# Attention scores as four products of 32 columns, with 128 columns kept for chunks on the diagonal

## The chip, the cores and the metric

The kernel runs on one core of a Trainium2 chip. The metric is the device time of one execution in microseconds, the median of several runs; less is better. The core has five engines that work at the same time and meet at semaphores: TensorE (PE in the profile; its weight loads are listed apart as PEld), VectorE (DVE), ScalarE (ACT), GpSimd (POOL) and SyncE (SP), whose queue issues most of the DMAs.

## What is computed

The reference is one layer of a decoder on x of 2 x 2048 x 512: attention, cross attention and a feed-forward net. The change lies in the attention. It has 16 heads of 32 in each of two batches, one set of queries, and two sets of keys and values, a short one with a bias and a long one without:

```python
scores = jnp.einsum('bhqd,bhkd->bhqk', q, k) / jnp.sqrt(jnp.float32(hd))
if bias is not None:
    scores = scores + bias[None, None]
attn = jax.nn.softmax(scores, axis=-1)
return jnp.einsum('bhqk,bhkd->bhqd', attn, v)
...
decay_bias = -jnp.abs(pos[None, :] - pos[:, None]) * (1.0 - decay_factor)
out_short = _attention(q, k_s, v_s, decay_bias)
out_long = _attention(q, k_l, v_l, None)
out = alpha * out_short + (1.0 - alpha) * out_long
```

## The kernel before

It runs in four parts, one after the other: `prepare` and `project` (norm, queries, keys and values, and the weights of the feed-forward net), `attend`, and `finish` (output projection, cross attention, feed-forward net). `attend` takes from about 490 us to 3670 us of the span.

`attend` works in **units**. A unit is one head with one set of keys and values: 32 heads in 16 passes of four units, w = 0 to 3. Even units (w = 0, 2) are the short attention with the bias, odd ones the long attention. The 2048 x 2048 scores of a unit are made twice, in f16 with the operands' high and low parts stacked along the contraction (96 rows, with rows for positions and maxima up to 103):

- `scores_for_max` (tile scores_qk, queries on the partitions): 16 tiles of 128 queries, 4 chunks of 512 keys each. VectorE reduces two chunks at a time to row maxima (line 983). Its 64 chunks c are numbered by 4 x tile + key chunk.
- `scores_for_exp` (tile scores_kq, keys on the partitions): 16 blocks of 128 keys, 4 chunks of 512 queries each. The row maximum is subtracted by a further row of the operands; ScalarE takes the exponential of each chunk into probs_T, in f32 (line 961).

`times_v` (line 1143) multiplies a finished block of probs_T by the values, in f32: four products of 32 columns for the four query chunks, each written to its own 32 partitions of outputs_T. The profile shows each f32 product as two records. GpSimd adds up the blocks for the row sums, some by an accumulating DMA; `count` (line 1150) sums them over the partitions by f32 products of 32 columns with ones.

The bias is linear in the positions on each side of the diagonal, with another sign above than below. So an even unit has two query operands, q_operand and q_operand_above (`q_up`), and a piece of a chunk takes the one for its side. `runs` (line 1068) splits a chunk into pieces: a chunk that lies on one side is one product of 512, and a chunk that holds a part of the diagonal has a piece to its left, the 128 x 128 piece on the diagonal, which takes q_operand, and a piece to its right. To the diagonal piece one further product with an identity (scores_qk) or two (scores_kq) add the kink. For tile or block t the diagonal lies in chunk t // 4, so 32 of an even unit's 128 chunks hold a part of it, none of an odd unit's.

The order on TensorE is written out in `one_pass` (line 1189). A unit has 16 **steps**. Step i does the values of block i, in steps 4 and 7 a count for the unit before, and then eight chunks of scores: one of scores_kq, two of scores_qk, two of scores_kq, two of scores_qk, one of scores_kq. The scores_kq chunks of step i are 4i + 7 to 4i + 10, counted on into the next unit from 64 on (`emitted`). The scores_qk chunks are the four of tile (i - 10) mod 16, of the unit after in steps 0 to 9 and of the one after that in steps 10 to 15 (`chunks_of`). scores_kq has three banks in PSUM, scores_qk two pairs of banks; TensorE waits for a bank at lines 1086 and 1089 (VectorE) and 1114 (ScalarE).

The row maxima of the next unit come together in step 10: VectorE reduces and negates them and turns them into rows (line 997), after the first reduction of that step. `place_max` on SP (line 767) then issues the DMAs that write them into the operand rows: eight of 1 KB for an even unit (four for q_operand, four for q_operand_above), four for an odd one. The first scores_kq chunk of the next unit, which is the second scores_kq chunk of step 14, waits for them at line 1120. In an odd unit's steps the next unit is an even one, with eight DMAs.

## Time and profile before

| | us |
|---|---|
| median of 3 runs | 4794.77 |
| lowest and highest | 4790.95 to 4795.98 |
| the profiled execution | 4789.35 |
| its span, first to last instruction | 4787.3 |

The profile is of one execution. Its page lists busy time by engine, the span in 40 equal slices of 120 us (busy tenths, and the granted clock of TensorE in tenths of full speed), the chain that ended last, and the costliest groups of instructions. A timeline gives the start in us, the time to the end of the group, the engine, line, operation and tiles, and how many records are merged; "96*128 96x512" is 96 rows and 128 columns of the stationary operand and 96 x 512 of the moving one, so 128*32 is a product of 32 columns. Records of products are pipelined: they overlap, and the distance between starts is what counts. Starts in a timeline are rounded to 0.01 us.

### The profile page before, as it was taken

To read this page: it belongs to the slowest core of one execution; us is meant where nothing else is said; L and a number is where in the kernel's file an instruction comes from. 1 tells how busy PE (TensorE), PEld (TensorE's weight loads), DVE (VectorE), ACT (ScalarE), POOL (GpSimd) and SP (SyncE) were. 2 spreads that over 40 slices of the span, in tenths; PEclk is the share of its full clock that TensorE was granted. 3 is DMA by queue.
4 is the path that set the end of the run, shared out by engine and by line. 5 is a ranking of instruction groups with operands and counts; after the bars stand their busy time and mean duration, and the time that the engine had idled before them with its cause. 6 is when DMAs were issued, how large, how long until landed. Compare 5 with 4: busy or idle time off the path is not lost. (4 is left out here: it accounts for less than half of the span.)

```text
span 4787.3 us, 95755 instructions
## 1 busy us (share of the span) xinstructions
PE 4623.8 (97%) x30732; PEld 2081.9 (43%) x30732; DVE 3784.0 (79%) x4400; ACT 2984.2 (62%) x5297; POOL 3069.2 (64%) x1236
## 2 busy tenths in 40 slices
PE   8999899999999999999999999999996899999998
PEld 3444233333333333333333333333331677777776
DVE  7657788888888888888888888888881688888887
ACT  3222377777777777777777777777774455555554
POOL 0000388888888888888888888888886233333332
PEclk9999799999999999999999999999998899999999
DMA  5444366766666666767676666666665000000000
GB/s 168 136 126 128 81 147 134 152 137 147 139 147 144 140 144 141 150 137 152 138 150 134 148 143 146 141 143 145 139 131 126 20 21 27 28 25 24 27 23 12
DMA packets 241866, 543.48 MB, mean 114 GB/s; under 512 B 71471, under 2 KB 145327, under 8 KB 200561
## 3 DMA queue, kind: packets, MB, share of 16 engines
q0 software_dynamic: 45792, 333.47, 35.3%
q1 hardware_dynamic: 195563, 203.94, 15.1%
q8 instruction: 258, 4.23, 0.4%
q14 instruction: 215, 1.76, 0.1%
q10 hardware_dynamic: 38, 0.08, 0.0%
HBM read 140.34 MB, written 62.16 MB: 42 GB/s over the span
## 5 line engine op out<-in xcount | busy, mean ns | idle before, releaser
L983 DVE TENSOR_REDUCE rowmax_parts<-scores_qk 128x1 f32<-128x1024 f32 x2048 | 2411.4, 1218 | 549.3 <-PE scores_qk L1066 547.7
L961 ACT ACTIVATE probs_T<-scores_kq 128x512 f32<-128x512 f32 x3840 | 2072.9, 600 | 622.7 <-PE scores_kq L1066 562.1
L868 POOL TENSOR_TENSOR probs_added<-probs_added,probs_T 128x2048 f32<-128x2048 f32 x446 | 2077.1, 4657 | 47.8 <-POOL probs_added L868 44.9
L1066 PE MATMUL scores_kq<-q_operand,k_operand 103*128 103x512 f16 (+3 forms) x3712 | 1175.9, 349 | 20.2 <-DMA q_operand_above<-negmax_T 10.4
L1143 PE MATMUL outputs_T<-probs_T,v_operand 128*32 128x512 f32 x7680 | 1024.7, 605 | 1.0 <-ACT probs_T L961 0.7
L1066 PE MATMUL scores_qk<-k_operand,q_operand 96*128 96x512 f16 (+4 forms) x3712 | 985.7, 349 | 22.4 <-DMA v_operand<-v_dram 14.6
L1066 PEld LDWEIGHTS scores_kq<-q_operand,k_operand 103*128 103x128 f16 x3712 | 350.3, 96 | 1022.4 <-ACT probs_T L961 643.0
L868 POOL TENSOR_TENSOR probs_added<-probs_T 128x2048 f32<-128x2048 f32 x64 | 290.7, 4543 | 349.2 <-ACT probs_T L961 349.2
L1751 PE MATMUL f_gate_up<-w_gate_up,xq_T 128*128 128x256 f16 (+1 forms) x4608 | 494.4, 266 | 7.7 <-DVE hidden L1642 6.5
L1066 PEld LDWEIGHTS scores_qk<-k_operand,q_operand 96*128 96x128 f16 (+1 forms) x3712 | 354.2, 98 | 304.4 <-DVE rowmax_parts L983 41.6
L1751 PEld LDWEIGHTS f_gate_up<-w_gate_up,xq_T 128*128 128x128 f16 x4608 | 421.3, 98 | 77.0 <-issue 24.3
L1066 PE MATMUL scores_kq<-q_operand_above,k_operand 103*128 103x512 f16 (+3 forms) x1152 | 339.6, 344 | 1.0 <-ACT probs_T L961 1.0
L1066 PE MATMUL scores_qk<-k_operand,q_operand_above 102*128 102x512 f16 (+3 forms) x1152 | 329.7, 349 | 0.0
L892 POOL DMA_DIRECT2D probs_poured<-probs_T x318 | 276.3, 912 | 76.5 <-ACT probs_T L961 69.4
L1459 POOL TENSOR_TENSOR hidden_parts<-hidden_q,hidden_parts 128x768 f16<-128x768 f32 x64 | 97.9, 1530 | 349.9 <-ACT hidden_parts L1534 349.9
L1143 PEld LDWEIGHTS outputs_T<-probs_T,v_operand 128*32 128x32 f32 x7680 | 151.2, 108 | 355.9 <-ACT probs_T L961 310.0
L843 POOL MEMSET ones<- 128x32 f32 x1 | 0.1, 125 | 464.6 <-issue 464.6
L555 PE MATMUL products_p<-xn_T_parts,w_qkv_parts 128*128 128x512 f16 x1152 | 255.7, 382 | 1.7 <-DVE xn_T_parts L408 1.5
L1736 PE MATMUL f_down<-w_down,hidden_T 128*128 128x512 f16 x1056 | 244.1, 380 | 0.0
L1066 PEld LDWEIGHTS scores_kq<-q_operand_above,k_operand 103*128 103x128 f16 x1152 | 110.8, 96 | 204.1 <-ACT probs_T L961 83.5
L936 ACT COPY sums<-scores_kq 128x512 f32<-128x512 f32 x126 | 73.8, 585 | 159.6 <-PE scores_kq L1150 159.6
L555 PEld LDWEIGHTS products_p<-xn_T_parts,w_qkv_parts 128*128 128x128 f16 x1152 | 113.3, 99 | 136.1 <-issue 5.6
(173 smaller groups left out, 4507.4 us busy)
## 6 DMA issues: line engine op xcount, KB each, us to landing
probs_poured<-probs_T POOLq DMA_DIRECT2D x318, 1024.0 KB, 8.4
qk_parts_dram<-qk_parts SPq DMA_DIRECT2D x96, 256.0 KB, 2.9
q_operand<-qk_parts_dram SPq DMA_DIRECT2D x192, 128.0 KB, 6.4
k_operand<-qk_parts_dram SPq DMA_DIRECT2D x192, 128.0 KB, 5.4
v_dram<-v_heads SPq DMA_DIRECT2D x16, 1024.0 KB, 6.4
v_operand<-v_dram SPq DMA_DIRECT2D x64, 256.0 KB, 5.2
sums_inverse<-sums_inverse_dram SPq DMA_DIRECT2D x64, 256.0 KB
q_operand_above<-qk_parts_dram SPq DMA_DIRECT2D x96, 128.0 KB, 7.0
```

The lines of the kernel that those rows point to most:

```text
L555: last = nc.tensor.matmul(mm[:, m % 4, :], w_parts[:, a, c, m * P:(m + 1) * P], xT[:, u, c, b, :], start=c == 0 and a == b, stop=c == KT - ...
L843: nc.gpsimd.memset(ones[:, :], 1.0).then_inc(consts, 1)
L868: nc.gpsimd.tensor_tensor(total, first, block_of(w, b), ALU.add).then_inc(added.sem, 1)
L892: nc.gpsimd.dma_start(total, block_of(w, b), accum_op=ALU.add).then_inc(landed.sem, 16)
L936: nc.scalar.copy(sums[:, j, :], pb[:, COUNT_SLOTS[j] % BANKS, :]).then_inc(sums_out.sem, 1)
L961: nc.scalar.activation(block_of(w, kb)[:, qt * BANK:(qt + 1) * BANK], pb[:, ring_of(c) % BANKS, :], ACT.Exp).then_inc(expd.sem, 1)
L983: nc.vector.reduce_max(rowmax[:, w % 2, g // 2, g % 2:g % 2 + 1], half, AX.X).then_inc(maxed.sem, 1)
L1066: return nc.tensor.matmul(out, lhsT, rhs, start=start, stop=stop, skip_group_check=True)
L1143: last = nc.tensor.matmul(po[qt * HD:(qt + 1) * HD, :], v_op[:, w, kb, :], block_of(w, kb)[:, qt * BANK:(qt + 1) * BANK], start=kb == 0, s ...
L1459: nc.gpsimd.tensor_tensor(h16[:, 1, a:a + w], hq[:, a:a + w], h16[:, 0, a:a + w], ALU.subtract)\
L1736: last = nc.tensor.matmul(pd[:, :], hT[:, c, a, :], wd[:, c, b, :], start=opens and c == first and a == b, stop=ends and c == first + coun ...
L1751: last = nc.tensor.matmul(pg[:, k % 2, g, 0:w], xqT[:, n % 2, c, a, :], w_up[:, c, g, b, at:at + w], start=c == 0 and a == b, stop=c == KT ...
```

## The change

`score` takes the number of columns, 32 if nothing is said, and issues one product for each 32 columns of the stationary operand, each to its own 32 partitions of the bank, as `times_v` does with its four. A chunk that holds a part of the diagonal is issued with 128 columns, as before, and so are its kinks. `runs` now gives such a chunk as two pieces, with the diagonal piece joined to the left one (scores_qk) or to the right one (scores_kq), the side that has the same query operand, and the kinks follow behind both pieces. The semaphore goes up at the last product of a chunk or of two, as before.

```diff
--- before.py
+++ after.py
@@ -1062,18 +1062,23 @@
             pe.wait_ge(consts, 2)
             pe.wait_ge(rows[0], 16 * 7)
 
-            def score(out, lhsT, rhs, start, stop):
-                return nc.tensor.matmul(out, lhsT, rhs, start=start, stop=stop, skip_group_check=True)
-
-            def runs(tile, chunk):
+            def score(out, lhsT, rhs, start, stop, columns=HD):
+
+                for j in range(0, P, columns):
+                    mm = nc.tensor.matmul(out[j:j + columns, :], lhsT[:, j:j + columns], rhs, start=start, stop=stop,
+                                          skip_group_check=True)
+                return mm
+
+            def runs(tile, chunk, with_left):
 
 
                 r = tile - chunk * NQ
                 if r < 0:
-                    return [(0, NQ, 1)]
+                    return [(0, NQ, 1)], None
                 if r >= NQ:
-                    return [(0, NQ, -1)]
-                return [x for x in ((0, r, -1), (r, 1, 0), (r + 1, NQ - 1 - r, 1)) if x[1]]
+                    return [(0, NQ, -1)], None
+                left = r + with_left
+                return [x for x in ((0, left, -1), (left, NQ - left, 1)) if x[1]], r
 
             def scores_for_max(w, n, c):
 
@@ -1092,13 +1097,14 @@
                     last = score(bank, q_op[w][0:PARTS3, t * P:(t + 1) * P],
                                  k_op[w][0:PARTS3, kc * BANK:(kc + 1) * BANK], True, True)
                 else:
-                    for i, (r, m, side) in enumerate(runs(t, kc)):
+                    sides, diagonal = runs(t, kc, 1)
+                    for i, (r, m, side) in enumerate(sides):
                         q = (q_up if side > 0 else q_op)[w]
-                        out = bank[:, r * P:(r + m) * P]
-                        last = score(out, q[0:MROW, t * P:(t + 1) * P],
-                                     k_op[w][0:MROW, kc * BANK + r * P:kc * BANK + (r + m) * P], i == 0, side != 0)
-                        if side == 0:
-                            last = score(out, ident16[:, :], kinkA[:, :], False, True)
+                        last = score(bank[:, r * P:(r + m) * P], q[0:MROW, t * P:(t + 1) * P],
+                                     k_op[w][0:MROW, kc * BANK + r * P:kc * BANK + (r + m) * P], i == 0, diagonal is None,
+                                     HD if diagonal is None else P)
+                    if diagonal is not None:
+                        last = score(bank[:, diagonal * P:(diagonal + 1) * P], ident16[:, :], kinkA[:, :], False, True, P)
                 if c % 2:
                     last.then_inc(scoredA.sem, 1)
 
@@ -1124,14 +1130,16 @@
                 if w % 2:
                     last = score(bank, k, q_op[w][0:MROW + 1, qt * BANK:(qt + 1) * BANK], True, True)
                 else:
-                    for j, (r, m, side) in enumerate(runs(kb, qt)):
+                    sides, diagonal = runs(kb, qt, 0)
+                    for j, (r, m, side) in enumerate(sides):
 
                         q = (q_up if side < 0 else q_op)[w]
-                        out = bank[:, r * P:(r + m) * P]
-                        last = score(out, k, q[0:MROW + 1, qt * BANK + r * P:qt * BANK + (r + m) * P], j == 0, side != 0)
-                        if side == 0:
-                            for part in range(2):
-                                last = score(out, ident16[:, :], kinkB[:, part, :], False, part == 1)
+                        last = score(bank[:, r * P:(r + m) * P], k, q[0:MROW + 1, qt * BANK + r * P:qt * BANK + (r + m) * P],
+                                     j == 0, diagonal is None, HD if diagonal is None else P)
+                    if diagonal is not None:
+                        for part in range(2):
+                            last = score(bank[:, diagonal * P:(diagonal + 1) * P], ident16[:, :], kinkB[:, part, :],
+                                         False, part == 1, P)
                 last.then_inc(scoredB.sem, 1)
 
             def times_v(w, n, kb):
```

## Rows read from the trace of the kernel before

**Rows 1.** The page: busy time, clock by slice, two of the costliest groups.

```profile
PE 4623.8 (97%) x30732; PEld 2081.9 (43%) x30732; DVE 3784.0 (79%) x4400; ACT 2984.2 (62%) x5297; POOL 3069.2 (64%) x1236
...
PEclk9999799999999999999999999999998899999999
...
L983 DVE TENSOR_REDUCE rowmax_parts<-scores_qk 128x1 f32<-128x1024 f32 x2048 | 2411.4, 1218 | 549.3 <-PE scores_qk L1066 547.7
...
L1143 PEld LDWEIGHTS outputs_T<-probs_T,v_operand 128*32 128x32 f32 x7680 | 151.2, 108 | 355.9 <-ACT probs_T L961 310.0
```

**Rows 2.** Waits of TensorE, 550 to 3610 us: waiter, cause, us, times, longest.

```profile
PE scores_kq L1066 <- DMA q_operand_above<-negmax_T: 5.9, 8, 1.2
...
PE outputs_T L1143 <- issue: 0.5, 2, 0.3
```

**Rows 3.** Timeline of TensorE, one step of an odd unit: start, us, instructions.

```profile
2000.25 1.07 PE L1143 MATMUL outputs_T<-probs_T,v_operand 128*32 128x512 f32 x8
2001.25 0.39 PE L1066 MATMUL scores_kq<-q_operand,k_operand 103*128 103x512 f16 x1
2001.48 0.60 PE L1066 MATMUL scores_qk<-k_operand,q_operand 96*128 96x512 f16 x2
2001.91 0.60 PE L1066 MATMUL scores_kq<-q_operand,k_operand 103*128 103x512 f16 x2
2002.35 0.59 PE L1066 MATMUL scores_qk<-k_operand,q_operand 96*128 96x512 f16 x2
2002.78 0.38 PE L1066 MATMUL scores_kq<-q_operand,k_operand 103*128 103x512 f16 x1
2003.09 1.07 PE L1143 MATMUL outputs_T<-probs_T,v_operand 128*32 128x512 f32 x8
```

**Rows 4.** Timeline of TensorE at the end of attention, the last row sums.

```profile
3663.47 3.62 PE L1150 MATMUL scores_kq<-probs_T,ones 128*32 128x512 f32 x32
3666.91 1.04 PE L1150 MATMUL scores_kq<-probs_added,ones 128*32 128x512 f32 x8
3667.77 1.04 PE L1150 MATMUL scores_kq<-probs_poured,ones 128*32 128x512 f32 x8
```

**Rows 5.** Timeline of TensorE in the last stage, 4011 to 4016 us.

```profile
4011.02 0.61 PE L1723 MATMUL f_hidden_T<-identity_f,hidden_parts 128*128 128x128 f16 x8
4012.55 3.67 PE L1677 MATMUL f_logits<-wo_sb,attn_T 128*128 128x512 f32 x8 [0.92 <-DVE x_out L1612]
4016.06 0.38 PE L1751 MATMUL f_gate_up<-w_gate_up,xq_T 128*128 128x256 f16 x2
```

**Rows 6.** Timeline of TensorE, a scores_kq chunk on the diagonal.

```profile
2042.67 0.33 PE L1066 MATMUL scores_kq<-q_operand_above,k_operand 103*128 103x384 f16 x1
2042.84 0.22 PE L1066 MATMUL scores_kq<-q_operand,k_operand 103*128 103x128 f16 x1
2042.89 0.28 PE L1066 MATMUL scores_kq<-kink_kq,ident_f 128*128 128x128 f16 x2
```

**Rows 7.** Timeline of VectorE, step 10 of an odd unit.

```profile
1997.74 0.15 DVE L997 STREAM_TRANSPOSE negmax_T<-negmax 128x32 f16<-128x32 f16 x1
```

**Rows 8.** Line 767 after that turn, 1997 to 2008 us: durations, starts, landing.

```profile
L767 SPq DMA_DIRECT2D q_operand<-negmax_T x4: 577/648/1370, 1998.5 to 2000.5; - x4
L767 SPq DMA_DIRECT2D q_operand_above<-negmax_T x4: 591/800/1215, 2002.3 to 2005.3; - x4
...
DMA to landing us min/median/max: 1.7/3.7/6.3
```

**Rows 9.** Timeline of TensorE, step 14 of the same unit.

```profile
2007.15 0.60 PE L1066 MATMUL scores_qk<-k_operand,q_operand 96*128 96x512 f16 x2
2007.58 0.22 PE L1066 MATMUL scores_kq<-q_operand,k_operand 103*128 103x128 f16 x1
```

**Rows 10.** Timeline of TensorE, step 14 two units later.

```profile
2104.25 0.60 PE L1066 MATMUL scores_qk<-k_operand,q_operand 96*128 96x512 f16 x2
2104.95 0.23 PE L1066 MATMUL scores_kq<-q_operand,k_operand 103*128 103x128 f16 x1
```

## The prediction

> **What bounds the kernel now.** I read the page first: TensorE is busy for 97% of the span, VectorE for 79%, and the granted clock stands at nine tenths or more in all but two of the 40 slices, so at the level of 2.4 GHz [rows 1]. A busy TensorE need not be working, so next came the waits of TensorE in the attention stretch: of some 3060 us it waited 5.9 us for the DMA that places the row maxima, in eight places, and 0.5 us for instructions [rows 2]. So in this stage TensorE's own stream sets the time. The timeline of one step shows what that stream is made of [rows 3]: a value block at 2000.25, the first score product at 2001.25, then seven more, the next value block at 2003.09. The step is 2.84 us. The reader is to see that the score products between 2001.48 and 2002.78 stand 0.217 us apart (1.30 us for six spacings), but 0.31 us pass from the last one to the value block, and 1.00 us from that to the first score product.
>
> How long the block takes without neighbours of another form is seen at the end of attention, where only 32-column products follow each other: 32 records from 3663.47 to 3666.91, in groups of four, is 0.43 us for a group, and the next two stretches of eight agree (0.86 us each) [rows 4]. A value block has two such groups, 0.86 us. So the step holds 0.86 + 8 x 0.217 = 2.595 us of work and **0.245 us that goes with the two changes of form**: 0.09 us before the block (0.31 - 0.217), 0.14 us in and after it (1.00 - 0.86), 0.01 us on the second product (2001.48 - 2001.25 = 0.23). It is not the change of data type: in the last stage eight f32 products with 128 columns are followed by f16 ones after 3.51 us, 0.44 us each with the start after an idle included, so the last of them has no 0.1 us more [rows 5].
>
> **The change, part by part.** *Changes of form.* A chunk on the diagonal now stands as 128 columns among products of 32, so it brings its own two changes. Their places follow from the order of the work. A scores_kq block kb has its diagonal in chunk kb // 4, and step i issues chunks 4i+7 to 4i+10. In an even unit that is the second of a step's four in steps 0 and 1, the third in 2 to 5, the fourth in 6 to 9, the first in 11 to 14; the next even unit's blocks 0 and 1 fall on the second in steps 14 and 15 of the odd unit. scores_qk does tile (i - 10) mod 16: in odd units' steps 0 to 9 there is one on the diagonal in each, in even units' steps 10 to 15 too. Counted with neighbours: an even unit has one interruption in each of steps 0 to 10, one in 11 to 13 (the two diagonal chunks stand side by side), two in 14 and one in 15, 17 in all; an odd unit has one in 0 to 9, none in 10 to 13, one in 14 and 15, 12 in all. Before, each step had one pair of changes: 32 for two units. After, 29. The seven eighths of the chunks that become 32 columns wide thus remove only three pairs in 32.
>
> Before, a pair costs 0.245 us. After, leaving 128 columns costs the same 0.09 us, and 32 columns the 0.14 us less what belongs to the first f32 pass. The first product after a change was late by 0.01 us at 128 columns; the value block's in-and-after 0.14 us holds about 0.02 us more than the 0.12 us of the way back. For f16 at 32 columns I bound that start by 0.01 and 0.02 us, so a pair by 0.23 and 0.245 us. Two units: 32 x 0.245 = 7.84 us before, 6.67 to 7.11 us after, 0.73 to 1.17 us saved; I take the middle, 0.95 us, since neither row is nearer.
>
> *Fewer pieces.* The diagonal piece joins a neighbour: in two units 24 fewer products. A 384-column piece and a 128-column one take 0.17 + 0.05 us [rows 6], one of 512 takes 0.217 us, so 0.003 us each, 0.07 us for two units. With the changes of form that is 1.0 us for two units, 31 times: 31 us.
>
> *Pace of a score chunk.* Four 32-column products take the place of one, 224 of the 256 chunks of two units. No row has f16 products in that form. From below I bound the chunk by the shortest spacing of 512-column products, 0.215 us (2001.91 to 2002.35 is two of them, 0.44, with rounding) [rows 3]; from above by four load-and-multiply pairs at the densest rate in the trace, 0.39 us for seven spacings of transposes, 0.056 us each, 0.224 us for four [rows 5]. Those transposes are limited by their 128 columns at 2.4 GHz (0.053 us), so this end is far off; nearer are the 32-column f32 groups, at the pace of the 128-column ones (0.43 against 0.44 us) [rows 4, 5]. I take 0.217 us, no change. One ns is 224 x 31 = 6.9 us.
>
> *Who else is asked for more.* In a step without interruption (2.6 us) VectorE has two reductions of 1.218 us [rows 1], 2.44 us, so it still hides; without that cover such steps would be held at its pace and give back the rest. ScalarE, busy for 62% of the span, has more room. The added instructions cost nothing as long as TensorE's sequencer stays ahead; it was late 0.5 us in all [rows 2]. No DMA and no wait is moved.
>
> *What is late next.* The three saved pairs, and one more from even to odd, all lie in steps 10 to 13 of odd units, 4 x 0.245 us. Between these and step 14 there is a chain that doesn't get faster: VectorE turns the maxima at 1997.74 [rows 7], SP issues eight 1 KB DMAs, the last at 2005.3, none landing in under 1.7 us, so not before 2007.0 [rows 8], and the second scores_kq of step 14 (the first chunk of the next unit, line 1120) needs them; it ran at 2007.58 [rows 9], 9.84 us after the turn and at most 0.6 us after the landing. In another unit it already waited: 0.70 us from 2104.25 to 2104.95 where 0.43 is the rule [rows 9, 10]. Over 31 odd units the wait is 5.9 / 31 = 0.19 us, so the product comes 10.03 us after the turn on average. After the change TensorE would be there earlier by the changes around four value blocks, 4 x 0.245 = 0.98 us, less 0.12 us for the new change just before it, 0.86 us. The landing is between 9.3 us (2007.0) and 10.03 us after the turn; from the slack of 0.6 us at most and none where it waited I take 9.87 us as the mean. So the product goes 0.16 us earlier, not 0.86 + 0.19 us less waiting: of its 0.86 us only 0.16 us is kept, **0.7 us of the 1.0 us is given back as waiting**, 0.7 x 31 = 22 us. Behind it on TensorE's queue stand the rest of the step's scores, for which ScalarE and VectorE wait.
>
> Sum: -31 + 22 = -9 us. The profiled execution took 4789.35 us (span 4787.3), 5.4 us under the median of the runs, 4794.77; it would take 4780 us, and the median **4786 us**. About 0.2% (9.6 us) is what a measurement of this kernel can tell from no change, so this forecast lies just inside.
>
> **The rivals.** *The wait gives back less* (faster). If the chain's end moves with TensorE, since VectorE's turn follows a score product, or if the landing is shorter with another timing of the DMAs, the 31 us stay, 4795 - 31 = 4764 us, and 4757 us with the low end of a pair (1.17 + 0.07 = 1.24 us, 31 times). For it: in eight places of 31 alone a wait is seen. Against: eight issues in a row take 6.8 us after the turn [rows 8], and none of it depends on TensorE. 0.10.
>
> *Four pairs cost TensorE's issue* (slower). Place: each 32-column chunk, eight instructions in 0.217 us instead of two. At 0.224 us it costs 7 x 6.9 = 48 us, of which some 7 us are hidden in the wait of step 14: 4827 us. It decides from 0.218 us on (9 / 6.9 = 1.3 ns), and the time is over 0.2% slower from 0.220 us. At 0.222 us: 4815 us. For it: no f16 row in this form, and each group with a semaphore to wait for has more to decode. Against: f32 groups of four pairs already follow each other at 0.43 us with no gap [rows 4], and 0.5 us is all that TensorE waited for instructions [rows 2]. 0.18.
>
> *Weights not loaded ahead.* Groups of 32 columns in a row ran at 0.43 us [rows 4] although each of their loads is recorded with 0.108 us [rows 1], so these were hidden. By the rule of the Trainium skill (TensorE: Matmul & The Clock Gate, Part 3, The mechanism) a weight load overlaps running products only when its row group differs, and column tiles share theirs; by that rule every chunk would show its load. The trace of the value products disagrees; for f16 no row shows it. As a mechanism of this kernel it would put 0.108 us in front of 7168 chunks: +774 us, 5569 us. 0.03.
>
> **How the numbers follow.** Forecast 0.69, alone from 4773 (pair at 0.23 us, 0.216 us a chunk) to 4805 us (0.219 us). The range from 4765 to 4820 us leaves out most of the first rival, the far end of the second and the third. Faster by over 0.2%: 0.10 and about four tenths of the forecast's share, 0.39. Slower: 0.18, from the second and third rivals and the forecast's tail. Within: 0.43.
>
> **What would show it.** Right: value block to first score product 0.86 us where nothing is interrupted; steps 10 to 13 of odd units near 2.6 us, step 14 longer than before; the waits for the DMA of the maxima up from 5.9 us to some 25 us; each lone diagonal chunk with 0.09 us behind it and 0.12 us before it. Wrong: a spacing of groups away from 0.217 us, an odd unit under 47.3 us (the wait didn't grow), or changes that cost less after f16 groups than after f32 ones.

## The result, and the profile after

The changed kernel is **slower by about 1%**: 4844.18 us (median of 4 runs, 4839.06 to 4849.38) against 4793.63 us (the kernel before, here with a fourth run), a ratio of 1.0105 with a 95% interval of 1.009 to 1.012. That is 50 us more where the forecast had 9 us less, and above the range's end of 4820 us. The profiled execution spans 4837.1 us, 49.8 us more than before.

The page of the changed kernel, busy times and the queue of instruction fetches (packets, MB, share of 16 DMA engines):

```profile
PE 4613.3 (95%) x51468; PEld 2209.8 (46%) x51468; DVE 3797.4 (79%) x4400; ACT 3030.7 (63%) x5297; POOL 3086.4 (64%) x1236
...
q8 instruction: 420, 6.88, 0.6%
```

TensorE is *less* busy than in [rows 1], 95% for 97%, in a longer span: it is not its work that grew. The kernel before had this line for the same queue:

```profile
q8 instruction: 258, 4.23, 0.4%
```

Waits of TensorE from 550 to 3650 us, changed kernel (waiter, cause, us, times, longest):

```profile
PE scores_kq L1068 <- DMA q_operand_above<-negmax_T: 52.1, 31, 2.8
PE outputs_T L1151 <- issue: 8.8, 2, 4.6
```

The wait for the row maxima grew from 5.9 us in eight places [rows 2] to 52.1 us in all 31 odd units, and two waits for instructions appeared. Everything else that the forecast rests on can be read in one odd unit. First the turn of the maxima, then a quiet step:

```profile
2010.37 0.15 DVE L997 STREAM_TRANSPOSE negmax_T<-negmax 128x32 f16<-128x32 f16 x1
```
```profile
2009.93 1.03 PE L1151 MATMUL outputs_T<-probs_T,v_operand 128*32 128x512 f32 x8
2010.79 0.39 PE L1068 MATMUL scores_kq<-q_operand,k_operand 103*32 103x512 f16 x4
2011.01 0.61 PE L1068 MATMUL scores_qk<-k_operand,q_operand 96*32 96x512 f16 x8
2011.44 0.61 PE L1068 MATMUL scores_kq<-q_operand,k_operand 103*32 103x512 f16 x8
2011.87 0.61 PE L1068 MATMUL scores_qk<-k_operand,q_operand 96*32 96x512 f16 x8
2012.31 0.39 PE L1068 MATMUL scores_kq<-q_operand,k_operand 103*32 103x512 f16 x4
2012.53 1.04 PE L1151 MATMUL outputs_T<-probs_T,v_operand 128*32 128x512 f32 x8
```

The step is 2.60 us for 2.84 [rows 3]; the value block takes 0.86 us (2009.93 to 2010.79), two chunks of four products 0.43 us (2011.01 to 2011.44). What was to be saved here is saved. Then steps 14 and 15 of that unit:

```profile
2018.80 0.64 PE L1068 MATMUL scores_qk<-k_operand,q_operand 96*32 96x512 f16 x8
2021.05 0.39 PE L1068 MATMUL scores_kq<-q_operand,k_operand 103*128 103x512 f16 x1 [1.62 <-DMA q_operand_above<-negmax_T]
...
2022.50 1.94 PE L1151 MATMUL outputs_T<-probs_T,v_operand 128*32 128x512 f32 x8
2024.21 0.66 PE L1068 MATMUL scores_kq<-q_operand,k_operand 103*32 103x512 f16 x4
2024.64 1.08 PE L1068 MATMUL scores_qk<-k_operand,q_operand 96*32 96x512 f16 x8
2025.65 0.23 PE L1068 MATMUL scores_kq<-q_operand_above,k_operand 103*128 103x128 f16 x1
```

The product that needs the maxima starts at 2021.05, 10.68 us after the turn; before, it came 9.84 us after it [rows 7, 9]. The DMAs are issued no later than they were, the last one 7.6 us after the turn in both kernels [rows 8]; it is the landing that is late:

```profile
L767 SPq DMA_DIRECT2D q_operand_above<-negmax_T x4: 590/806/1325, 2014.9 to 2018.0; - x4
```

And behind the wait the work itself is slow: the value block at 2022.50 takes 1.71 us to the next product instead of 0.86. The windows over this stretch say why (PE, PEld, DVE, ACT, POOL busy; granted clock; DMA share; GB/s):

```profile
2020.00:2021.00 1.00, 0.00 (x0) 0.00 (x0) 0.71 (x1) 0.00 (x0) 1.00 (x1) 1.00 0.39 92
2021.00:2023.00 2.00, 1.95 (x23) 0.88 (x27) 0.63 (x1) 1.31 (x3) 2.00 (x3) 0.80 0.64 168
2023.00:2024.00 1.00, 1.00 (x8) 0.17 (x4) 0.59 (x1) 0.37 (x1) 1.00 (x1) 0.50 1.00 260
2024.00:2025.00 1.00, 1.00 (x12) 0.34 (x8) 0.00 (x0) 0.41 (x1) 1.00 (x1) 0.50 0.98 262
...
2026.00:2027.00 1.00, 1.00 (x23) 0.49 (x24) 1.00 (x2) 0.81 (x2) 1.00 (x1) 1.00 1.17 246
```

Behind an idle of 1.62 us the granted clock stood at 0.50, the level of 1.2 GHz, in the windows from 2023, and was back at 1.00 by 2026. In windows of 7 us from 9.5 us after each turn, units 5 to 59, the mean clock was below 0.95 in 9 of 28 (0.76 in the one above) and the loss adds up to 16 us of full-speed time; before, it stood at 1.00 in all 28.

Mean lengths from value block to value block, worked out from the two traces over units 4 to 59 (28 odd, 28 even):

```
                          before   after
odd, steps 0 to 13         42.05   41.16 us
odd, steps 14 and 15        6.15    8.41 us
even, all 16 steps         49.14   49.12 us
units 4 to 59 in all      2725.6  2763.2 us
units 60 and 61             99.7   109.6 us
```

So the odd units gain 25 us ahead of step 14 (0.89 x 28) and lose 63 us in steps 14 and 15 (2.26 x 28): together 38 us, which is the 37.6 us of units 4 to 59. Another 10 us are lost near the loop's end.

### The profile page after: what moved, and what is told of

It reads as the page before. It is cut to its first block and busy times, and to the rows that moved or that the text cites. A ratio compares the mean times of both kernels' runs of the same rounds, so it can differ in the third digit from the quotient of the medians.

```text
span 4837.1 us, 137227 instructions
## 1 busy us (share of the span) xinstructions
PE 4613.3 (95%) x51468; PEld 2209.8 (46%) x51468; DVE 3797.4 (79%) x4400; ACT 3030.7 (63%) x5297; POOL 3086.4 (64%) x1236
## 5 line engine op out<-in xcount | busy, mean ns | idle before, releaser
L961 ACT ACTIVATE probs_T<-scores_kq 128x512 f32<-128x512 f32 x3840 | 2115.1, 599 | 562.9 <-PE scores_kq L1068 495.5
L1068 PE MATMUL scores_kq<-q_operand,k_operand 103*32 103x512 f16 (+2 forms) x11776 | 1190.5, 381 | 70.8 <-DMA q_operand_above<-negmax_T 56.6
L1068 PE MATMUL scores_qk<-k_operand,q_operand 96*32 96x512 f16 (+3 forms) x11776 | 1046.1, 383 | 24.2 <-DMA v_operand<-v_dram 14.6
L1068 PEld LDWEIGHTS scores_qk<-k_operand,q_operand 96*32 96x32 f16 (+2 forms) x11776 | 352.1, 98 | 661.2 <-issue 403.0
L1068 PEld LDWEIGHTS scores_kq<-q_operand,k_operand 103*32 103x32 f16 (+1 forms) x11776 | 346.2, 96 | 645.2 <-ACT probs_T L961 268.9
L1068 PE MATMUL scores_qk<-k_operand,q_operand_above 102*32 102x512 f16 (+3 forms) x3456 | 366.2, 377 | 0.1
L1068 PE MATMUL scores_kq<-q_operand_above,k_operand 103*32 103x512 f16 (+3 forms) x3456 | 360.1, 369 | 0.7 <-ACT probs_T L961 0.3
L1151 PEld LDWEIGHTS outputs_T<-probs_T,v_operand 128*32 128x32 f32 x7680 | 227.9, 111 | 179.1 <-issue 10.6
L1068 PEld LDWEIGHTS scores_kq<-q_operand_above,k_operand 103*32 103x32 f16 (+1 forms) x3456 | 119.6, 96 | 285.5 <-ACT probs_T L961 100.3
L961 ACT ACTIVATE probs_poured<-scores_kq 128x512 f32<-128x512 f32 x256 | 140.1, 595 | 82.5 <-PE scores_kq L1068 82.3
```

The lines of the kernel that those rows point to most:

```text
L961: nc.scalar.activation(block_of(w, kb)[:, qt * BANK:(qt + 1) * BANK], pb[:, ring_of(c) % BANKS, :], ACT.Exp).then_inc(expd.sem, 1)
L1068: mm = nc.tensor.matmul(out[j:j + columns, :], lhsT[:, j:j + columns], rhs, start=start, stop=stop, skip_group_check=True)
L1151: last = nc.tensor.matmul(po[qt * HD:(qt + 1) * HD, :], v_op[:, w, kb, :], block_of(w, kb)[:, qt * BANK:(qt + 1) * BANK], start=kb == 0, s ...
```

## The experiments

Where the landing is told of, it is the time from the start of the turn of the maxima to the last semaphore step of the unit's eight DMAs, in the 28 odd units 5 to 59, worked out from the traces. Before: mean 9.75 us. After: 10.65 us. Each ratio is to runs of the kernel before made beside the experiment: 4795.07 us for experiments 1 to 4, 4792.36 us for 5 to 8, 4796.04 us for 9 to 12.

The fetch queue q8 was the suspect: the changed kernel has 137,227 instructions for 95,755, and 41,472 more instructions are 162 more packets of 256, just the 420 for 258 of the page. Each packet has 16,384 bytes and takes about 1 us; between 600 and 3500 us one began every 16.7 us before and every 9.1 us after (means from the traces). Theory A: these packets delay the maxima's DMAs. Theory B: the landing moves with the earlier products.

**1. More instructions in the kernel before.**

```diff
+                for _ in range(6 if rhs.shape[-1] == BANK else 0):
+                    pe.nop(nofuse=True)
```

> The kernel before, with six no-operation instructions on TensorE's queue behind every score product of 512 columns, as many instructions as the change adds, and no product changed. Theory A (code): the instruction queue q8 goes from 258 packets to some 420, one such packet then falls into nearly every transfer of 1 MB between the turn of the maxima and step 14, the eight DMAs land 10.3 to 10.9 us after the turn instead of 9.3 to 9.6, and TensorE's wait for them goes from 5.9 us to 20 to 30 us; with some 8 us at the two edges of the loop the time is 25 to 40 us over the kernel before. Theory B (timing): the wait comes from score products that are earlier against the transfers, which these instructions don't make; 5.9 us stays, and the time is within 5 us of the kernel before.

Measured: 4794.99 us, ratio 1.0005 (0.9995 to 1.0015), and still 258 packets and 95,755 instructions. The no-ops never entered the stream, so this tells nothing about either theory.

**2 and 3. The large accumulating DMAs moved by a block, in both kernels.** About 1 us after the turn, GpSimd issues a DMA that adds a block of 1 MB to probs_poured (line 892, the pour).

```diff
-BY_DMA = (1, 6, 9, 12, 15)
+BY_DMA = (1, 5, 8, 12, 15)
-BY_POOL = (3, 4, 5, 7, 8, 10, 11, 13, 14)
+BY_POOL = (3, 4, 6, 7, 9, 10, 11, 13, 14)
```

> The changed kernel, with the accumulating DMAs of blocks 5 and 8 in place of 6 and 9 (GpSimd adds 6 and 9 instead), so that the 1 MB transfer is over some 4 us earlier against the turn of the maxima. Theories A and B both: the wait for the maxima, 52 us, falls under 6 us, and with it the half clock behind the long waits; the time falls by 45 to 65 us, to 4780 to 4800 us. If the wait stays, the late landing is not due to that transfer and both fall. Under A some 9 us of waits for instructions at the edges of the loop stay.

> The kernel before with the same two accumulating DMAs moved: what the move is worth without the change. A and B: the 5.9 us of waits go, 4786 to 4792 us. The distance from this kernel to the changed one with the same move is what the change is worth without its late chain: by the prediction's counts -31 us, under A some 9 us less for the edges of the loop, so -22 us; under B -31 us.

Measured: the changed kernel 4941.95 us, ratio 1.0308 (1.0291 to 1.0325), the kernel before 4895.48 us, 1.0214 (1.0197 to 1.0231). Waits of TensorE, first in the changed kernel, then in the one before:

```profile
PE scores_kq L1068 <- ACT probs_T L961: 72.7, 55, 3.3
PE scores_kq L1068 <- DMA q_operand_above<-negmax_T: 39.1, 26, 2.8
```
```profile
PE scores_kq L1066 <- ACT probs_T L961: 66.2, 65, 4.5
PE scores_kq L1066 <- DMA q_operand_above<-negmax_T: 5.5, 8, 1.2
```

Both expectations missed: the pour stayed near the turn (issued at most 4 us before it and 2 us behind it in the 28 odd units), and the exponentials now waited for buffers that were still being poured: ScalarE waited 189.6 and 166.3 us for pours, 9 us in either kernel without the move. What can be kept is that the change costs 46 us here too (4942 - 4895), with the same pair of waits, 39.1 for 5.5 us.

**4 and 5. One iteration of a longer loop, in both kernels.**

```diff
-TURN = 7
+TURN = 14
```

> The changed kernel with all 14 middle passes written out in one turn of the loop instead of two turns of seven, so without the jump back near 2126 us, where TensorE waited 4.6 us for instructions. Theory A: that wait and the slow clock behind it are gone, -5 to -7 us, 4837 to 4840 us; the waits for the maxima stay at 50 us. If the wait was not the jump's, the time is the changed kernel's within 3 us.

> The kernel before with the loop's body of fourteen passes instead of seven, run once: the control for the same edit made to the changed kernel, which took 44 us off it (4844 to 4800), more than the loop's edges alone (about 10 us in the first block, about 4 at the exit). Theory C (the edges and the code's size cost only the kernel with the longer code): here the edit is worth 0 to 10 us, 4785 to 4797, and the waits of TensorE for the row maxima stay at about 6 us. Rival D (the edit is worth as much whatever the products): 4745 to 4760, the same 35 to 45 us, and then the change alone costs about 45 us in this form too.

Measured: the changed kernel 4800.24 us (ratio to the kernel before 1.0017, 1.0007 to 1.0027), the kernel before 4785.83 us (0.9981, 0.9971 to 0.9991). The edit is worth 44 us to the changed kernel, more than was expected of it, and 7 us to the kernel before, so theory C held and rival D fell. Why the changed kernel gained 44 us where some 6 were expected was only found in part, as follows. In this form the change costs 14 us, 0.3%. The maxima's wait is hardly touched, here in the changed kernel:

```profile
PE scores_kq L1068 <- DMA q_operand_above<-negmax_T: 48.4, 31, 2.4
```

Gone are the waits for instructions; units 60 and 61 take 97.4 us for 109.6. In the changed kernel with two iterations, the loop's jump back looks like this (timeline of TensorE):

```profile
2126.30 0.39 PE L1068 MATMUL scores_kq<-q_operand,k_operand 103*32 103x512 f16 x4
2131.33 1.89 PE L1151 MATMUL outputs_T<-probs_poured,v_operand 128*32 128x512 f32 x8 [4.64 <-issue]
```

The kernel before waited there for 0.26 us. Also, with a single iteration most register arithmetic falls away (122,493 instructions for 137,227). Units 4 to 59 take 2747.4 us for 2763.2; the wait at the jump is 4.64 of these 16 us, and what the fewer instructions bring of the rest wasn't separated.

**6. Every product in 32 columns.** With this no change of form is left in the attention (also with 14 passes).

```diff
-                                     HD if diagonal is None else P)
+                                     HD)
...
-                        last = score(..., ident16[:, :], kinkA[:, :], False, True, P)
+                        last = score(..., ident16[:, :], kinkA[:, :], False, True)
```

The kinks of scores_kq lose their `P` in the same way.

> The changed kernel with every score product and every diagonal piece in four of 32 columns, so that no change of form is left in the attention, and the body of fourteen passes. By the forecast's price of 0.245 us a pair, 29 pairs in two units and 32 times two units come to about 215 us gross; the wait for the row maxima takes a part back, as the odd unit's fourteen steps grow shorter by up to 2.9 us while the landing stays at 10.7 us: 60 to 90 us. So 4660 to 4740 against the 4800 of the same body with 128 columns on the diagonal chunks, with waits of TensorE for the row maxima of 100 to 140 us. Rival (the short pieces in four cost TensorE's issue more than the changes of form): 4790 or more, and the steps of the even units are no shorter than 3.07 us.

Measured: **4730.16 us**, ratio 0.986 (0.9844 to 0.9877), the fastest whole version. It is 114 us under the changed kernel, but 44 us of that are the edit of experiment 4; with the same body of fourteen passes it is 70 us under the changed kernel (4800.24) and 56 us, 1.2%, under the kernel before (4785.83). A diagonal chunk in this kernel (timeline of TensorE):

```profile
1977.87 0.60 PE L1068 MATMUL scores_qk<-k_operand,q_operand 96*32 96x512 f16 x8
1978.31 0.23 PE L1068 MATMUL scores_kq<-q_operand_above,k_operand 103*32 103x128 f16 x4
1978.36 0.33 PE L1068 MATMUL scores_kq<-q_operand,k_operand 103*32 103x384 f16 x4
1978.53 0.29 PE L1068 MATMUL scores_kq<-kink_kq,ident_f 128*32 128x128 f16 x8
1978.64 0.39 PE L1068 MATMUL scores_kq<-q_operand,k_operand 103*32 103x512 f16 x4
```

A piece of 128 columns takes 0.05 us as four products (1978.31 to 1978.36), as much as it took as one [rows 6], so the rival of the short pieces falls. The median of steps 0 to 9 of odd units is 2.66 us for 2.88 in the changed kernel, 0.21 us for the pair of changes that such a step had. Its waits:

```profile
PE scores_kq L1068 <- ACT probs_T L961: 61.8, 62, 4.5
PE scores_kq L1068 <- DMA q_operand_above<-negmax_T: 58.5, 31, 2.8
```

The landing has a mean of 10.91 us. The maxima's wait, expected at 100 to 140 us, is only 58.5 us, since new waits for ScalarE come ahead of it.

**7. More instructions that stay in the stream.** The kernel before, with three waits on risen semaphores twice over behind each 512-column product.

```diff
+                if rhs.shape[-1] == BANK:
+                    for done, value in ((consts, 2), (rows[0], 16 * 7), (cleared, 1)) * 2:
+                        pe.wait_ge(done, value)
```

> The kernel before, with about 12,100 more instructions in TensorE's stream in place of the change's 11,700 product and weight-load pairs: behind each 512-column score product it waits on three semaphores that have long risen. The products, their widths and the order are those of before. Theory A (the longer stream's fetches delay the row-maxima transfers): the fetch packets rise from 258 to about 340 (one packet to 256 instructions), the landing after the turn rises from a mean of 9.75 us to 10.0 to 10.4, late in 16 to 24 of the 28 odd units of the loop instead of 10, TensorE's wait for it from 6 us to 12 to 35 us, and the time to 4800 to 4830. Theory B (the wait came because the products are earlier against an unchanged transfer): packets rise, landing and wait stay at 9.75 us and 6 us, the time at 4788 to 4799. Rival (the sequencer is the bound): idle time of TensorE put down to issue grows by over 20 us, with the maxima's wait unchanged.

Measured: 5004.29 us, ratio 1.043 (1.0412 to 1.0448). There are 21,504 more instructions, not the 12,100 of the expectation, and so 342 packets, as it says. But the waits themselves slowed TensorE: a step like that of [rows 3] now takes 3.47 us.

```profile
2096.67 1.06 PE L1147 MATMUL outputs_T<-probs_T,v_operand 128*32 128x512 f32 x8
...
2100.14 1.06 PE L1147 MATMUL outputs_T<-probs_T,v_operand 128*32 128x512 f32 x8
```

TensorE then came later than the maxima, and the wait for them fell to 1.8 us, so this run can't test what theory A says of the wait and the time. It can test the landing, and there A's numbers missed too: the mean was 9.60 us where 10.0 to 10.4 was expected, and 10 of 28 units landed after 9.8 us, not 16 to 24. Unit by unit the packets show all the same: the 16 units in which one began 0.4 to 7.5 us after the turn landed at 9.88 us, the other 12 at 9.22 us. None began at 7.5 to 8.7 us, where the landings of the other runs are latest (below).

**8 and 10. Without the pour beside the transfers.** The pour of block 9 moves 64 columns instead of 2048, in the changed kernel and in the one before. The other columns of that block are missing from the row sums.

```diff
-                nc.gpsimd.dma_start(total, block_of(w, b), accum_op=ALU.add).then_inc(landed.sem, 16)
+                columns = 64 if b == 9 else NQ * BANK
+                nc.gpsimd.dma_start(total[:, :columns], block_of(w, b)[:, :columns], accum_op=ALU.add).then_inc(landed.sem, 16)
```

> The changed kernel with the pour of block 9, the one that lies beside the row-maxima transfers of the odd units, cut from 2048 to 64 columns; its other columns are left out of the row sums. Instruction fetches stay (420 packets). Theory A (a fetch packet and the pour in one engine's queue delay the last maxima transfers): the landing goes back to 9.3 us or less after the turn, TensorE's wait for it from 52 us to under 6 us, no half clock in step 14, and the time to 4785 to 4805; what is left above 4786 is the loop's edges (about 14 us). Theory B (an earlier need against the same transfer): landing 10.4 to 10.8, wait 45 to 55 us, 4838 to 4850.

> The kernel before with the pour of block 9 cut from 2048 to 64 columns, as was done to the changed kernel (which came to 4756 us); the other columns are left out of the row sums. If the forecast's gross gain (31 us of changes of form) is right and only the landing of the row maxima ate it: here the maxima's waits go from 6 us to none, 4780 to 4792, and the difference between the two kernels without that pour is the forecast's 31 us within 5 (units 4 to 59 of the first block 2715 to 2722 us here, 2693 there). Rival (the pour cost the kernel before as much): 4750 to 4765, and the change is worth nothing even without the pour.

Measured: the changed kernel **4756.37 us**, ratio 0.9921 (0.9905 to 0.9938); the kernel before 4784.60 us, 0.9978 (0.9968 to 0.9987). Neither waits for the maxima any more in units 5 to 59. The first lines of TensorE's waits, changed kernel, then the one before:

```profile
PE scores_kq L1069 <- ACT probs_T L962: 12.0, 18, 6.2
PE outputs_T L1152 <- issue: 5.2, 2, 2.6
```
```profile
PE scores_kq L1067 <- ACT probs_T L962: 9.0, 17, 4.6
PE outputs_T L1144 <- issue: 0.6, 2, 0.3
```

The landing is 7.46 and 7.23 us. Without that pour the change brings 28 us (4784.60 - 4756.37); in units 4 to 59 it is 2719.3 to 2693.3 us, 26 us. The pour costs the kernel before 6 us there (2725.6 - 2719.3) and the changed one 70 us (2763.2 - 2693.3). So the 26 us are the forecast's gain, and the 64 us by which the pour costs the changed kernel more are what took it back. The expectation for 10 held, and its rival (the pour cost both the same) falls. For 8, theory B falls; theory A had the direction right, but the kernel came out 29 us under A's range, and the landing under its 9.3 us. What 8 and 10 show is that the loss needs the pour. They don't show that it needs the packets: without the pour the landing came well ahead of the product that needs it in either kernel (by 1.5 us after the change, by 2.6 us before, on average), though nearly every odd unit of the changed kernel still had its packet.

**9. Half a packet.** The kernel of experiment 5 with 128 pairs of waits, each pair one instruction, ahead of TensorE's first products of the attention; nothing else is moved.

```diff
             pe.wait_ge(rows[0], 16 * 7)
+            for _ in range(128):
+                pe.wait_ge(cleared, 1)
+                pe.wait_ge(consts, 2)
```

> The kernel before with the body of fourteen passes, and 128 waits on long risen semaphores ahead of TensorE's first product of the attention: half of a 256-instruction fetch packet, so that every later packet boundary lies half a packet earlier in the program; all products and their order are unchanged. Without the 128, the landing after the turn was 9.07 to 9.59 us in each odd unit from 15 to 41, where no fetch packet started from 1 us before to 9.6 us after the turn, and 9.86 to 11.13 us in most of the units 5 to 11 and 43 to 59. Theory A (a fetch packet beside the pour delays the last transfers): the late landings change places: at least 8 of the 14 odd units 15 to 41 land after 9.8 us, and most of the units 5 to 11 and 47 to 57 before 9.6 us. Theory B (the landing follows the products, not the fetches): the same units are late as before. Either way 4780 to 4795 us, within 0.2% of the kernel without the 128.

Measured: 4785.41 us, as without them (4785.83), with one packet and 128 instructions more. The late units changed places. Of the 14 odd units 15 to 41, eight now land after 9.8 us (15 and 21 to 33); all of 5 to 11 and 47 to 57 land before 9.6 us. One unit shows it on both sides. Unit 53 without the 128 instructions, turn at 3162.24. The first fence is the DMA view from 1 us before the turn to 9.5 us behind it, fetch packets and the median landing of the second four maxima DMAs; the second is who waited for line 767's transfers:

```profile
q8 instruction: 1, 0.02, 0.5%
...
q_operand_above<-negmax_T SPq DMA_DIRECT2D x4, 1.0 KB, 3.4
```
```profile
who waited for it (us, times):
  PEld scores_kq L1066: 1.7, 1
  PE scores_kq L1066: 1.2, 1
```

With them, the same unit's turn is at 3165.85; the DMA view of the same stretch has no line for q8, the four DMAs take 2.6 us, and the timeline of TensorE goes on without a wait:

```profile
q_operand_above<-negmax_T SPq DMA_DIRECT2D x4, 1.0 KB, 2.6
```
```profile
3175.26 0.60 PE L1069 MATMUL scores_qk<-k_operand,q_operand 96*128 96x512 f16 x2
3175.69 0.22 PE L1069 MATMUL scores_kq<-q_operand,k_operand 103*128 103x128 f16 x1
```

Unit 25 does the reverse: no packet and no wait without the 128, a packet and this row of the timeline with them:

```profile
1813.79 0.23 PE L1069 MATMUL scores_kq<-q_operand,k_operand 103*128 103x128 f16 x1 [0.55 <-DMA q_operand_above<-negmax_T]
```

The products, their order and their widths are the same, only the packets' places differ. Theory A is shown for the kernel before (eight late units are just the number that was asked for), theory B falls there. The landings of the runs with the pour in its place or cut short, by whether a fetch packet began 2 to 9.6 us after the turn, a window chosen after the traces were seen (units, mean us):

```
                                with      without
before                        10, 10.34  18,  9.43
before, no-ops (1)            10, 10.34  18,  9.41
before, 14 passes              8, 10.53  20,  9.37
before, 14, half a packet      7, 10.44  21,  9.28
after                         27, 10.69   1,  9.62
after, 14 passes              25, 10.67   3, 10.00
all 32 columns, 14 passes     24, 11.04   4, 10.12
before, more waits (7)        15,  9.76  13,  9.41
before, short pour            10,  7.65  18,  7.00
after, short pour             27,  7.46   1,  7.56
```

Where the pour itself was moved, the same window doesn't always sort the landings. In experiment 3 it does (10.22 us with a packet, 9.26 us without), in 11 too (10.29 and 9.02 us, three units without), in 2 one unit alone has no packet (10.25 and 10.35 us), and in 12 the order is reversed (8.59 and 9.37 us).

The place of the packet inside the window matters as well. Where one began 7.5 to 8.7 us after the turn, about when the last of the eight DMAs is issued, the mean landing was 10.63, 10.60 and 10.56 us in the kernel before (as it was, with 14 passes, with half a packet; 4 units each) and 10.75 and 10.68 us in the changed kernel (23 units, and 17 with 14 passes). Where one began 0.4 to 7.5 us after the turn instead, it was 10.13 to 10.24 us in the three and 10.21 and 10.17 us in the two. At the same place of the packet the two kernels thus land within 0.2 us of each other. The change took the units with a packet there from 4 to 23.

**11 and 12. The pour later, nothing left out.**

```diff
-POOL_ORDER = (1, 4, 5, 6, 7, 8, 9, 10, 11, 12, 13, 14, 15)
+POOL_ORDER = (1, 4, 5, 6, 7, 8, 10, 9, 11, 12, 13, 14, 15)
```

> The changed kernel, whole, with the pour of block 9 issued behind GpSimd's add of block 10 instead of ahead of it, some 5 us later, so that it pours behind most of the row-maxima transfers of the odd units. Theory A (packet and pour together make the landing late): the landing falls from 10.66 us to 8 to 9.3 us, the maxima's wait from 52 us to under 10 us, and the time to 4755 to 4795 (the edges of the loop stay or go with it). Rival (the late pour holds the block's buffer, and the exponentials wait for it): new waits on probs_T of 30 us and more, and 4840 or above.

> The kernel with every score product in four of 32 columns and the body of fourteen passes (4730 us, with waits of 59 us for the row maxima and 62 us for probs_T), with the pour of block 9 behind the add of block 10. Theory A: the maxima's wait falls to 25 us or less, the waits for probs_T stay, and the time is 4685 to 4710. Rival (the exponentials wait for the buffer held longer): waits on probs_T grow by as much as is gained, 4725 or above.

Measured: 5059.32 us (1.055, 1.0524 to 1.0575) and 5001.52 us (1.043, 1.0412 to 1.0447). In the changed kernel with the later pour, ScalarE and GpSimd wait for pours, 9.0 and 6.8 us before the move:

```profile
ACT probs_T L961 <- DMA probs_poured<-probs_T: 235.3, 99, 7.1
```
```profile
POOL probs_poured L892 <- DMA probs_poured<-probs_T: 279.8, 79, 8.0
```

The rival held in both: the buffer kept longer costs more than an earlier landing brings. Theory A's own numbers missed in 11 (landing 10.15 us, wait for the maxima 52.2 us); in 12 the wait fell to 22.0 us, as A had it. No way to use experiment 8's gain with the whole computation was found.

## Why the prediction was wrong

- **The gross gain held.** Forecast 1.0 us for two units from changes of form and pieces. Measured without the pour: 26 us in 28 pairs of units, 0.93 us. Its main part lies where it was put: odd units' steps 10 to 13 went from 2.84 to 2.60 us, the even units stayed (49.14 and 49.12 us). The reading of the clock ahead of it was slightly off: three of the 40 slices, not two, stand below nine tenths [rows 1]; nothing in the sum hangs on it.
- **A pair of changes** was taken as 0.23 to 0.245 us after f16 groups. Experiment 6 shows 0.21 us in steps 0 to 9 of odd units, a small miss; it would have added to the gain, which came out at 0.93 us all the same.
- **The pace held**: 0.43 us for two chunks, 0.217 us each. So the rival of TensorE's issue (4827 us) was not the cause, though its sign came true. The weights are loaded ahead in f16 as well: four loads of 0.096 to 0.098 us each are on record for each chunk of 0.217 us. The rule of the Trainium skill (TensorE: Matmul & The Clock Gate, Part 3, The mechanism), by which column tiles would show their loads, doesn't agree with this spacing.
- **The place of the loss was right, its size was not.** The forecast had the wait for the row maxima in step 14 take back 0.7 us per odd unit, 22 us, with the landing held at 9.87 us after the turn because "no DMA and no wait is moved". TensorE did come to that product 0.84 us earlier than before, 9.07 us after the turn for 9.91 (means of the 28 odd units; forecast 0.86 us). But the landing went from 9.75 to 10.65 us, and the product started 10.78 us after the turn where it had been 10.06 us (the forecast had 9.87 for 10.03). Measured against experiments 8 and 10 the step gave back 64 us in 28 odd units, 2.3 us each; the forecast's 0.7 us make 20 us of them.
- **The step that failed** is "the added instructions cost nothing as long as TensorE's sequencer stays ahead", and with it "no DMA and no wait is moved". The sequencer did stay ahead but for some 10 us. Yet the added instructions bring DMA traffic of their own: the profile lists their fetches (q8) among the packets of the 16 DMA engines, beside the pour and the maxima. A packet beside the transfers, in 10 of 28 odd units before, is there in 27 of 28 after, with a mean landing of 10.69 us. So the product that needs the maxima came 0.72 us later than before, where the forecast had it 0.16 us earlier: 0.88 us, or 25 us in 28 units. The forecast had no term for it.
- **A second term was missing**: the half clock. In 9 of the 28 units the work behind the wait ran at 1.2 GHz for some 3 us, which cost 16 us. So the 64 us are some 20 of the forecast's own term, 25 of the later landing (together the 44 us by which the wait for the maxima grew in these units, 47.9 for 4.2 us), 16 of the clock, and 3 that were not found.
- **A third**: the loop's jump back and its exit, 4.6 and 4.2 us of waits for instructions where it was 0.5 us in all [rows 2]. The Trainium skill (Runtime: NRT & Kernel Launch, Instruction fetch mechanics) has such stalls at branches taken out of what is loaded; the row at 2131.33 agrees. But in experiment 8, with the same instructions, the two took 5.2 us together and units 60 and 61 99.6 us, so the length of the code alone doesn't fix the price. That was left open.

How a packet delays the last transfer isn't shown. A packet takes about 1 us, and each of the maxima's DMAs is done only with the last of 16 semaphore steps, so a packet that holds up one step would be enough; but the traces don't tell through which engine a packet went. The same section of the Trainium skill gives 256 instructions to a fetch of 16 KB, which 41,472 = 162 x 256 bears out. It calls the cost of crossing into the next fetch mostly hidden; TensorE's waits for instructions in the attention, 10.7 us, agree with that but for the 8.8 us at the loop's edges. Units with a packet beside the transfers landed 0.9 to 1.2 us later, though (kernel before, as it was and with 14 passes), and that landing is what TensorE waits for in step 14.

For the changed kernel itself the packets were not taken away with the products kept. There theory A rests on the comparison by the packet's place, in which at most some 0.2 us of the mean landing are left for another cause, and on the shift shown in experiment 9 for the kernel before; experiment 8 adds only that the pour is needed.

## What to carry to other kernels

More instructions are more DMA traffic: count their fetch packets (256 instructions each) as transfers, and look at which small transfer with a deadline shares the DMA engines with them. A landing time is not a constant of a DMA, above all while a large transfer runs, so a wait that barely hides now is the first place to put a loss. If half a rewrite leaves mixed forms behind, try the whole one: with the body of fourteen passes throughout, the diagonal chunks at 32 columns as well brought 1.2% where this change lost 0.3%.

## What the runs showed of the hardware that was not expected

- Shifting the program by 128 instructions moved the late landings to other units (experiment 9), at the same total time.
- Nine of the 28 waits of TensorE in the changed kernel, of 1.62 to 2.85 us, were followed by some 3 us or more at half the granted clock; eight others of 1.7 to 2.25 us were not, nor were the shorter ones, and the waits before the change (0.9 us at most in these units) had none.
- Four 32-column products on 128 columns of moving data took 0.05 us together, no more than one of 128 (experiment 6).
- Waits on semaphores that had long risen were not free on TensorE: 21,504 more instructions in experiment 7, each with two such waits, cost 212 us, 10 ns each.
